# Mamba in a decoder layer: the filter tile is written state by state, and three layer norm roots change their slots

## The reference

```python
xb = silu(causal_conv4(in_proj(rmsnorm(x))))
delta = softplus(xb @ xp_w[:16] @ dtw + dtb);  Bm, Cm = xb @ xp_w[16:48]
dA = exp(delta * -exp(a_log));  mi = delta * Bm * xb
v = 0.6 * v + mi            # for each time step, channel and state
h = dA * h + v
y = sum over the states of h * C
y = (y + dp * xb) * silu(z);  x = x + out_proj(y)
```

## Time and profile before

| | |
|---|---|
| median of 3 runs | 1756.39 us |
| the profiled execution | 1755.87 us |
| its span, first to last instruction | 1754.6 us |
| granted TensorE clock, mean | 0.964 |
| Mamba part (first v to last added tile) | about 70 to 1136 us |
| busy: PE, DVE, ACT, POOL | 89%, 67%, 47%, 57% |

### The profile page before, as it was taken

How to read it: one execution, slowest core, us unless ns; L and a number is a source line. 1 busy time by engine, 2 the same in 40 slices (tenths; PEclk the granted TensorE clock), 3 DMA queues, 4 the chain that set the end, 5 groups by cost and what they waited for, 6 DMA issues and landing times.

```text
span 1754.6 us, 23969 instructions
## 1 busy us (share of the span) xinstructions
PE 1553.2 (89%) x8962; PEld 1171.2 (67%) x8962; DVE 1176.9 (67%) x1890; ACT 824.4 (47%) x1151; POOL 1006.1 (57%) x821
## 2 busy tenths in 40 slices
PE   5698899999999899899899898758988888899998
PEld 2477778878877778787788788733343443667676
DVE  3477878777876886886786879827666673243334
ACT  3656536537547546546645643402546467311110
POOL 2468867967976976976976988763030300014441
PEclk9999999999999999999999999977999999899999
DMA  4000100100010001001000112044250500601224
GB/s 175 22 25 26 49 25 26 49 25 25 25 49 26 25 32 42 25 25 49 25 25 28 70 49 97 1 99 82 60 109 1 96 1 1 247 25 63 63 67 162
DMA packets 38116, 92.80 MB, mean 53 GB/s; under 512 B 9137, under 2 KB 21937, under 8 KB 33521
## 3 DMA queue, kind: packets, MB, share of 16 engines
q1 hardware_dynamic: 29392, 73.68, 13.1%
q0 software_dynamic: 7584, 16.53, 3.7%
q10 hardware_dynamic: 1024, 1.05, 0.3%
HBM read 64.88 MB, written 9.57 MB: 42 GB/s over the span
## 4 chain that ended last, share of the span: by engine, by line
PE 62%; DVE 12%; POOL 11%; issue 7%; ACT 6%; SPq 1%; DMA 1%; DVEq 0%; ACTq 0%; POOLq 0%
PE psum L450 14%; POOL hst L750 7%; PE psum L431 7%; PE psum L387 4%; DVE hst L577 4%; PE psum L1456 4%; PE psum L1441 4%; PE psum L1035 3%; DVE uw L479 3%; PE psum L422 3%; PE psum L1017 2%; PE psum L411 2%; POOL uw L714 2%; PE psum L393 2%; PE psum L1394 2%
## 5 line engine op out<-in xcount | busy, mean ns | idle before, releaser
L750 POOL TENSOR_TENSOR hst<-hst,cb 128x512 f32<-128x512 f32 x512 | 647.5, 1292 | 241.1 <-DVE hst L577 239.7
L577 DVE TENSOR_TENSOR_SCAN hst<-dA,psum 128x256 f32<-128x256 f32 x512 | 321.9, 670 | 136.3 <-PE psum L450 108.5
L577 DVE TENSOR_TENSOR_SCAN hst<-dA,hst,psum 128x256 f32<-128x256 f32 x512 | 352.7, 730 | 83.5 <-PE psum L450 80.2
L431 PE MATMUL psum<-ident,hst 128*128 128x128 f32 x2048 | 312.0, 276 | 34.3 <-POOL hst L750 33.7
L450 PE MATMUL psum<-filt,uT 128*128 128x172 f32 (+1 forms) x1536 | 270.6, 313 | 20.9 <-DVE hst L577 20.9
L431 PEld LDWEIGHTS psum<-ident,hst 128*128 128x128 f32 x2048 | 253.3, 142 | 48.3 <-POOL hst L750 46.8
L450 PE MATMUL psum<-filt,c_early 128*128 128x172 f32 (+1 forms) x1536 | 269.5, 312 | 12.5 <-DVE hst L577 11.4
L450 PEld LDWEIGHTS psum<-filt,c_early 128*128 128x128 f32 x1536 | 235.5, 192 | 51.7 <-issue 26.3
L450 PEld LDWEIGHTS psum<-filt,uT 128*128 128x128 f32 x1536 | 234.5, 192 | 53.1 <-DVE hst L577 28.5
L690 ACT ACTIVATE dA<-delta,alog 128x512 f32<-128x512 f32 x256 | 176.8, 719 | 177.4 <-DVE hst L577 177.3
L690 ACT ACTIVATE dA<-xres,alog 128x512 f32<-128x512 f32 x256 | 176.8, 718 | 146.0 <-DVE hst L577 145.9
(11 more groups left out here) (205 smaller groups left out, 2007.9 us busy)
## 6 DMA issues: line engine op xcount, KB each, us to landing
cb<-c_rows SPq DMA_DIRECT2D x32, 1024.0 KB, 4.7
qk<-part SPq DMA_DIRECT2D x120, 64.0 KB, 2.4
qk<-part POOLq DMA_DIRECT2D x72, 64.0 KB, 4.7
w_up<-up_dram SPq DMA_DIRECT2D x8, 512.0 KB, 8.3
w_down<-down_dram SPq DMA_DIRECT2D x8, 512.0 KB, 13.5
w_up<-y_choice SPq DMA_DIRECT2D x8, 512.0 KB, 7.8
xm<-x_dram SPq DMA_DIRECT2D x4, 512.0 KB, 9.2
w_early<-w_in_dram SPq DMA_DIRECT2D x2, 1024.0 KB, 9.1
```

The lines of the kernel that those rows point to most:

```text
L431: m = pe.matmul(psum[:, Y0 + et, t * P:(t + 1) * P], hst[:, i % NH, t * P:(t + 1) * P], ident[:], start=n == 0 and t == 0, stop=n == NSTAT ...
L577: dve.tensor_tensor_scan(h[:, t0:t0 + HS], dA[:, st % NDA, t0:t0 + HS], bank("v", i)[:, n * HS:(n + 1) * HS], h[:, t0 - 1:t0] if t0 else 0 ...
L750: pool.tensor_tensor(h, h, cb[:, q % 2, state_of(i)[1] % GN, :], ALU.mult).then_inc(g_done, 1)
```

## The change

**Filter.** `pool_filter` gets a second argument n, the state in the group, and writes only that state's part, 6 x 86 = 516 elements in each partition, with a stride between the chunks. It is called ahead of tiles 0, 4, 8 and 12 of the group before, for n = 0, 1, 2, 3. The waits stand at n = 0 alone; `filt_done` rises with n = 3. The first filter of all is made by four such instructions in a row.

**Norms.** In `plan_norms` the roots move from the slot of the aggregate to one (part 0) or two (part 1) slots behind it, into the slot of the reciprocal; part 1 as a whole begins at slot 46, where it was slot 48. In `plan_attention` the root moves two slots, from slot 42 into the reciprocal's slot 44, and the three scales stand in slots 46, 48 and 50, where they were in 45, 46 and 47.

```diff
@@ plan_norms
                 put("dve", "x_aggr", g)
+                s += 1 + g
                 put("act", "x_roots", g)
-                s += 1
                 put("dve", "x_rec", g)
@@ plan_attention
                 put("dve", "ln2_aggr")
+                s += 2
                 put("act", "ln2_root")
-                s += 2
                 put("dve", "ln2_rec")
                 for b in range(B - 1):
-                    s += 1
+                    s += 2
                     put("dve", "ln2_scale", b)
@@ the plan
-                    plan_norms(k, TILES - 16, 1)
+                    plan_norms(k, TILES - 18, 1)
@@ pool_filter
-            def pool_filter(f):
+            def pool_filter(f, n):
                 k, g = f // NG, f % NG
-                if f == 0:
-                    pool.wait_ge(ld_scan, 48)
-                pool.wait_ge(bank_dve, emptied_by("dve", k, "dbcT", 0))
-                if f >= 2:
-                    pool.wait_ge(v_full, GN * ET * (f - 1))
-                pool.tensor_tensor(filt[:, f % 2], toep[:, :].unsqueeze(1).unsqueeze(1).to_broadcast([P, NCH, GN, QC]),
-                                   bcol[:, k % 2, :, g * GN:(g + 1) * GN].unsqueeze(3).to_broadcast([P, NCH, GN, QC]),
-                                   ALU.mult).then_inc(filt_done, 1)
+                if n == 0:
+                    if f == 0:
+                        pool.wait_ge(ld_scan, 48)
+                    pool.wait_ge(bank_dve, emptied_by("dve", k, "dbcT", 0))
+                    if f >= 2:
+                        pool.wait_ge(v_full, GN * ET * (f - 1))
+                i = pool.tensor_tensor(filt[:, f % 2, :, n, :], toep[:, :].unsqueeze(1).to_broadcast([P, NCH, QC]),
+                                       bcol[:, k % 2, :, g * GN + n].unsqueeze(2).to_broadcast([P, NCH, QC]), ALU.mult)
+                if n == GN - 1:
+                    i.then_inc(filt_done, 1)
@@ pool_mamba
-                pool_filter(0)
+                for n in range(GN):
+                    pool_filter(0, n)
                 for i in range(NI * TILES):
                     q = i // (GN * ET)
+                    if i % ET == 0 and q + 1 < NI * NG:
+                        pool_filter(q + 1, i // ET % GN)
                     if i % (GN * ET) == 0:
-                        if q + 1 < NI * NG:
-                            pool_filter(q + 1)
                         pool.wait_ge(ld_c[q % 2], 16 * (q // 2 + 1))
```

## The result

The changed kernel takes 1764.25 us (median of 7 runs, 1758.79 to 1770.07), the kernel before, timed beside it, 1756.39 us (7 runs, 1752.40 to 1759.76). The ratio is 1.0044, with a 95% interval from 1.0028 to 1.0060: it is slower by some 8 us, where 1.7 was forecast. The time lies within the range of 1749 to 1766, near its upper end. The ratio lies past the bound of 0.3% that the prediction set for "no change", with the lower end of the interval just inside it. The profiled execution took 1764.57 us, its span is 1763.1 us (before: 1755.87 and 1754.6).

What follows compares the result with a forecast made beforehand. TensorE was busy 89% and 62% of the chain, GpSimd counting only where ahead of it. Terms +5.4 - 0.5 - 1.0 - 2.2 = +1.7 us on 1755.9 gave 1757.6, put at 1758; range 1749 to 1766.

Steps and rivals of the forecast that it cites:

- The price of a piece: GpSimd's time for one of the four pieces of a filter: 1.06 us, bounds 0.90 and 1.27.
- d: Delay one piece adds on GpSimd, taken as 1.02 us since consecutive records overlap by about 0.04.
- Passes 2 to 5: Pieces at slots 40 and 44 make slot 48's v 1.81 us late, 0.46 comes back: +1.35 each, +5.4.
- The sign I gave for it: TensorE idle some 0.8 us before the v of slot 48, released by GpSimd's filter, in every pass from 1 to 6.
- The waits at slots 37 and 53: TensorE's idle times behind the filter there, 1.39 and 0.24 us before, would be gone.
- Passes 1 and 6: Product of slot 36 starts 1.59 us earlier, then +1.35 from the later pieces: net -0.24 each, -0.5.
- Pass 0: Slot 48's v waits 4.2 us, covered by TensorE's 5.22 us idle for ScalarE's copy; earlier roots help: together -1.0.
- the uncovered case: First pass: if the 4.2 us wait for slot 48's filter is not covered by TensorE's idle time, +3.2.
- Pass 7: Shorter filter waits by slot 12, shorter residual add at slot 34, moved root and scales: -2.2, bounds -7 and +1.
- A: Rival: the pieces hide, those of slots 40 and 44 cost nothing: -9.2, 1747 us; chance 0.22.
- B: Rival: late filter, dearer pieces (1.27 us) delay slot 48's v, first pass's wait uncovered: +10, 1766 us; chance 0.23.
- C: Rival: norm half does nothing, second root still in its products' slot: +0.5 to +1, 1758.5 us; chance 0.55 together with forecast.

Runs made afterwards that it cites:

- group2_early: Changed kernel, but in each pass's third group (slots 32 to 47) the pieces stand ahead of tiles 0, 4, 4, 4; 1749.41 us, ratio 0.9968.
- placed: Changed kernel, but pieces put, by pass and group, where traces show GpSimd idle, partly ahead of the group's own start; 1744.05 us, ratio 0.9947.
- second profile: The changed kernel run once more, nothing altered; 1764.39 us, ratio 1.0044.
- filter_only: Changed kernel with the norms of the kernel before, so only the filter is in pieces; 1768.13 us, ratio 1.0070.
- last_at_40: Changed kernel, but in each pass's third group the pieces stand ahead of tiles 0, 4, 4, 8 (last at slot 40); single run, 1754.22 us.

## Why the prediction was right, and where it was not

**The price of a piece** was right: a median of 1.064 us, forecast 1.06, and d = 1.02 is what the add of slot 46 was late by (+1.02 of the 2.89 at slot 46, 1.87 being the later start of the pass). The mean of 1.122 holds eight pieces that took 1.50 to 2.05 beside instructions of VectorE.

**Passes 2 to 5** were right by mechanism and nearly by size: v of slot 48 came 1.93 us late (forecast 1.81), 0.39 was given back (0.46), and a pass is 1.53 longer (1.35). The four make +6.1 for +5.4. The experiments show every part of the term: +1.0 for the piece in the gapless stretch (forecast 1.02), +0.97 for the late one (0.79 by the forecast, 1.81 less 1.02), and -0.44 with neither (group2_early against before; 0.46). The working has two slips: the gapless stretch holds 12 products, not 10, on which nothing hangs, and the end of a product is put at 586.12 and then at 586.17, which is worth 0.05 us. The sign I gave for it, some 0.8 us of idle time before the v of slot 48, was there as 0.73 wherever the clock stayed full: in passes 5 and 6 of the first profile and 2 to 5 of the second. Elsewhere TensorE's slower matmuls stood in its place; in pass 3 of the first profile 0.26 us of idle time were left. The waits at slots 37 and 53 are gone, as forecast.

**Passes 1 and 6** are the step that failed. I took 1.59 us of gain, because GpSimd's product would start when the scans allow, and 1.35 of loss. Of the gain some 0.85 went back at once: VectorE's max, which has two SBUF inputs, begins while the piece of slot 36 runs. It takes 1.54 us here and 0.70 in the kernel before, and the scans behind it are that much later. The row before, then the row after:

```profile
296.46 0.70 DVE L502 TENSOR_TENSOR xres<-xres,xraw 128x512 f32<-128x512 f32 x1 [0.99 <-ACT xraw L664]
```

```profile
296.01 1.54 DVE L502 TENSOR_TENSOR xres<-xres,xraw 128x512 f32<-128x512 f32 x1 [1.00 <-ACT xraw L664]
```

The piece as such is not to blame for that: in placed nothing stands at slot 36, a product runs there, and the max takes 1.55 us beside it. I had put the cost of GpSimd coming earlier into VectorE's way at nothing.

1.53 - 1.59 + 0.84 = 0.78 is what the first profile has for each of the two passes. In the second profile, and in filter_only, the clock's fall adds some 1.7 to each, and they are +2.5. For the two passes together that is +1.6 to +5.0, where -0.5 was forecast.

Each of these falls comes behind an add that waited some 1.95 us for its product; the piece at slot 40 adds its 1.02 to a wait that was 0.93 before. Over passes 1 to 6 of all profiles of this study that wait was 1.94 to 1.96 us in 23 passes, and the clock fell behind it in 10 of them. In the other 49 it was 1.54 once and at most 0.94 else, no wait in slots 42 to 49 was longer than 1.54, and the clock stayed full behind it. So the falls go with the long wait, but the wait alone does not decide: last_at_40 waits as long in passes 1 and 6, keeps full clock and has 133.15 and 133.08, and the changed kernel itself does both. TensorE of last_at_40 in pass 1, at the place where 1.58 us were shown above for the six matmuls:

```profile
309.44 0.66 PE L431 MATMUL psum<-ident,hst 128*128 128x128 f32 x4 [1.94 <-POOL hst L758]
309.93 1.03 PE L450 MATMUL psum<-filt,uT 128*128 128x172 f32 x6
```

What decides it stays open. This step with the larger value takes the sum from "no change" to "slower": I had looked for TensorE's idle times and not asked what they do to its clock.

**Pass 0** was covered, as forecast: 4.12 us of wait for the filter cost 0.2 to 0.5 us and not 3.2. But it was not 1.0 shorter. The copy still came late by 1.42 and then 0.54, so the cover was used up and nothing was left over. Without the norm half it was the uncovered case: filter_only has +3.3, forecast for that case +3.2.

**Pass 7** gained 3.1 us for 2.2, by terms that were partly others. By slot 12 the v's were 1.6 us earlier, as forecast. The v of slot 48 then waited 1.47 us for its late piece, for which I had nothing in this pass. The filter alone gave 2.1 of the 3.1, the norm half the rest. The residual add fell from 6.05 us to 4.39, as the forecast's "under 4.5" has it, and it still waited through three GpSimd instructions, a piece and two products. VectorE, then GpSimd, in pass 7 of the changed kernel:

```profile
1082.35 4.39 DVE L546 TENSOR_TENSOR xres<-xres,xm 128x1024 f32<-128x1024 f32 x1
...
1098.41 1.94 DVE L546 TENSOR_TENSOR xres<-xres,xm 128x1024 f32<-128x1024 f32 x1
```

```profile
1082.15 1.06 POOL L729 TENSOR_TENSOR filt<-toep,bcol 128x516 f32<-128x516 f32 x1
1083.17 2.50 POOL L753 TENSOR_TENSOR hst<-hst,cb 128x512 f32<-128x512 f32 x2
...
1096.77 2.50 POOL L753 TENSOR_TENSOR hst<-hst,cb 128x512 f32<-128x512 f32 x2 [2.07 <-DVE hst L577]
1099.23 2.04 POOL L729 TENSOR_TENSOR filt<-toep,bcol 128x516 f32<-128x516 f32 x1
```

The page "SBUF — State Buffer" of the Trainium skill, section "Who interferes with whom", lets the loser wait for a whole instruction. The third add agrees with it: it began beside a product that ran to 1099.27, and the piece behind that product took 2.04 us. The first add agrees only as with a lower bound, since it lost to three in a row.

**The rivals.** A, that the pieces hide, falls: they don't hide at slots 40 and 44. With these two pieces out of the way the Mamba part is 5.2 us shorter than before (group2_early), not 9.2. That placed is 10.2 shorter is no support for that price: it also moves pieces in passes 0 and 7. B, the late filter, names the right place; its price for a piece was too high, and its uncovered pass 0 came only without the norm half. That its 1766 is close to what was measured is luck. C, that the norm half does nothing, holds in the Mamba part for it alone (+0.1) and not beside a filter that comes late (-3.7) or well placed (-2.9).

**The sum.** By the first two profiles, 8.7 us apart: passes 2 to 5 +6.1, passes 1 and 6 +1.6, pass 0 +0.2, pass 7 -3.1; the rest, +3.9, lies before and behind the Mamba part, where it is spread and no term. By the second profile of the changed kernel: +6.1, +5.0, +0.5, -3.1, in all +8.6, near what the timed medians show (+7.9 and +8.9). That the time fell into the range is in part luck: the range reached up to 1766 for dearer pieces and an uncovered pass 0, neither of which came, and TensorE's clock, which brought the time there, was no term of it. It was also stated that the runs of one kernel spread by 3 us; the seven runs of the kernel before spread over 7, those of the changed kernel over 11.

## What to carry to other kernels

A producer's deadline is not the slot in which its consumer's work is used but the one in which it is issued: count the lead, and put pieces of it where the engine is idle, pass by pass, since here the same 128 pieces made 1764 us or 1744 by their places alone. Before a cost is put into a gapless stretch, ask who follows that engine, and whether the idle time it makes in a dense stream of matmuls may also cost clock. Two halves of a change can be each other's cover, so they are to be tried apart and together.

## What was not expected of the hardware

- One wait of 1.96 us in place of 0.93 was followed by a fall of TensorE's clock in 10 passes of 23. The granted clock of the 7 us around it in pass 1 was 0.76 in the first profile of the changed kernel and 0.56 in the second, and the same program had a pass of 133.96 us once and of 135.69 the other time. What decides between the two is not settled here. First profile, then second (the window starts 0.8 and 0.4 us behind the start of the add that waited):

```profile
311.50:318.50 7.00, 6.62 (x41) 6.11 (x41) 3.91 (x7) 3.67 (x6) 7.00 (x7) 0.76 0.00 0
```

```profile
313.00:320.00 7.00, 6.31 (x30) 5.84 (x29) 3.53 (x6) 2.35 (x4) 7.00 (x7) 0.56 0.00 0
```

- A piece of 516 elements took 2.04 to 2.05 us for 1.05 in seven places: six beside VectorE's clip (L499, one input, 2048 elements, 1.92 us), one beside a residual add (L546, two inputs). Of such a pair now the one and now the other is stretched: in pass 7 the first residual add took 4.39 us beside pieces and products of usual length, the third 1.94 beside a piece of 2.04.
- The part behind the Mamba part, unchanged in all kernels here, spreads over 8 us between single profiles. A difference of one profile in a part that the change does not touch says nothing below that.
